# A decoder layer on one core: the state products of a chunk issued beside the output products of the chunk before it

## The chip, the cores and the metric

The kernel runs on one NeuronCore of a Trainium2 chip. The time is device microseconds of one execution; the time before is the median of three runs. A trace of one profiled execution shows every instruction of the engines: TensorE (PE, with its weight loads as PEld), VectorE (DVE), ScalarE (ACT), GpSimd (POOL), and SyncE, which starts the DMAs.

## The reference

The layer works on x of shape (4, 1024, 256): four batches, 1024 tokens, 256 channels. Its first part is a gated linear attention with 16 heads of 16 channels, whose core is a recurrence over tokens (q, k, v, beta and g come from projections of the normalised input, a rotating scan and short convolutions):

```
def step(Sst, inp):
    qt, kt, vt, bt, gt = inp
    Sd = gt[..., None, None] * Sst
    kS = jnp.einsum('bhk,bhkv->bhv', kt, Sd)
    Snew = Sd + jnp.einsum('bhk,bhv->bhkv', kt, bt[..., None] * (vt - kS))
    ot = jnp.einsum('bhk,bhkv->bhv', qt, Snew)
    return (Snew, ot)
```

The output o is normalised, gated and projected, and added to the input. The second part is a differential cross-attention over 64 context tokens. The third is a depthwise and a pointwise convolution, a mixture of 8 experts of which each token takes 2 (all 8 are computed), a normalisation and a small feed-forward layer.

## The kernel before

The 1024 tokens are worked through in 8 blocks of 128 tokens (of all four batches at once). A block passes through two halves. The first half holds projections and the recurrence; the second half holds cross-attention, experts and feed-forward. They are overlapped: the program runs through turns i from -2 to 8, and in turn i it does the recurrence of block i, the second half of block i-1 and the projections of blocks i+1 and i+2. Turns 1 to 6 are alike and are called steady here. Turn 0 has the recurrence but no second half; turn 8 has a second half alone.

The order of work on each engine is written out by hand in the table ORDERS, one list of steps for each engine and kind of turn ("head" for turns up to 0, "steady", "drain" for turn 7, "last" for turn 8). A word such as z.3 is a step with its arguments; a prefix tells the block: none is block i, - is block i-1, + is block i+1, * is block i+2. Every engine does its list strictly in order, and a step waits for semaphores of other steps: `up(name, n)` waits until event name has been counted n times, `fin` counts one. A further table, KEEP, gives how many filler products (128x128, two instructions each, into a bank that nobody reads) TensorE issues ahead of a step; they are left out while a projection is half done in the filler's bank.

The recurrence is done in 8 chunks of 16 tokens. For chunk c:
- PE z.c (L1934) forms products of the solved triangle with keys and queries in banks 2 and 3, and DVE zc.c (L1405) puts them into slot c % 4 of zc_ring.
- PE d1.c (L1951) multiplies keys with the state of the chunk before, in banks 0 and 1, and DVE m.c (L1415) makes rq, slot c % 2, from it and the values.
- PE cs.c (L1967), the state products, go to banks 0 and 1 in two halves, cs.c.0 and cs.c.1. A product takes 32 rows and 64 columns of the array. Half 0 uses the row quarters 0 and 2, half 1 the quarters 1 and 3, in both column halves: eight products or 16 instructions on four pieces of the array. Two row quarters mustn't write one bank at a time, so half 1 waits for the end of half 0. DVE s.c (L1422, four instructions) then makes the new state, for which d1.(c+1) waits.
- PE co.c (L1983), the output products, have the same shape and two halves in banks 2 and 3. They wait until zc has read z.(c+3) from these banks and until o.(c-1) is done. DVE o.c (L1433 and three at L1436) sums them up. z.(c+4) waits for o.c.

So a chunk has four halves one after another: co.(c-1).0, co.(c-1).1, cs.c.0, cs.c.1, with other work between some of them.

Other steps that the text speaks of: PE pv and DVE av (attention), PE wp and DVE wp (L1550, projection of the attention), turn4 (a turn by TensorE, copied by ScalarE), DVE dconv (L1564, L1569, depthwise convolution) for PE pw, router, PE moe.0 to moe.31 (L2132, experts, with a bias product at L1700), ScalarE moe (L1037), DVE acc (L1634, weighted sum over the experts), turn5, mi and mo (their output projection), hnorm (ScalarE L1046, L771, L772, then DVE L1644), turn6, ffd and ffu (feed-forward), turn1 (L1784, the input of block i+2 turned; copies L801 and L1229), and onorm, og, wo (output of the recurrence).

Of the kernel before, what the change touches and what calls it, by code (L numbers as in the profile page):

```python
# [105 lines left out]
def steps(words):  # L106

    out = []
    for word in words.split():
# [13 lines left out]
        -pt.12 -pt.13 -pv.6.0 -pv.6.1 -turn3.0 -pt.14 -pt.15 -wp.0.0 -wp.0.1 -pv.7.0 -pv.7.1 cs.0.0 cs.0.1 z.2
        +proj.3.0 z.3 d1.1 co.0.0 co.0.1 cs.1.0 cs.1.1 -turn4.0 z.4 d1.2 co.1.0 co.1.1 cs.2.0 cs.2.1 +proj.3.1 z.5
        d1.3 co.2.0 -turn3.1 -wp.1.0 co.2.1 cs.3.0 cs.3.1 +proj.4.0 +proj.4.1 z.6 d1.4 co.3.0 co.3.1 cs.4.0 +proj.5.0
        +proj.5.1 cs.4.1 -wp.1.1 -pw.0.0 -pw.0.1 z.7 -turn4.1 d1.5 -router.0 -moe.0 co.4.0 co.4.1 -moe.1 -pw.1.0
        cs.5.0 -pw.1.1 -moe.2 -moe.3 -router.1 -moe.4 -moe.5 -moe.6 -moe.7 -moe.8 -moe.9 -moe.10 -moe.11 -moe.12
        cs.5.1 -moe.13 -moe.14 -moe.15 -moe.16 -moe.17 -moe.18 -moe.19 -turn5.0 -moe.20 -mo.0.0 -mo.0.1 -moe.21
        -moe.22 -moe.23 -moe.24 -moe.25 -moe.26 -moe.27 -moe.28 -moe.29 co.5.0 -moe.30 -moe.31 -mi d1.6 co.5.1
        -turn5.1 cs.6.0 cs.6.1 *turn1.0 *turn1.1 co.6.0 d1.7 co.6.1 cs.7.0 cs.7.1 co.7.0 co.7.1 -turn6.0 -mo.1.0  # L130
        -mo.1.1 -ffd.0 -turn6.1 -ffu.0 -ffd.1 onorm.0 *rot.0 onorm.1 wo.0 *rot.1 wo.1 *gate.0 wo.2 -ffu.1 *unrot
        +sum.0 +sum.1'''),
        "dve": steps('''
        dsel.0 -ln2.0.0 -ln2.0.1 -ln2.1.0 -ln2.1.1 -max.0.0 -max.0.1 dsel.1 norm.0 gsub.0 gsub.1 norm.1 norm.2.0
        norm.2.1 -max.1.0 -max.1.1 norm.3.0 norm.3.1 am.0 am.1 +cond am.2 am.3 solve.0.0 -av.0.0 -av.0.1 solve.0.1
        solve.1.0 solve.1.1 solve.2.0 -av.0.2 -av.0.3 -max.2.0 -max.2.1 +db -av.1.0 -av.1.1 -av.1.2 -av.1.3 -max.3.0
        -max.3.1 -av.2.0 -av.2.1 solve.2.1 -av.2.2 -av.2.3 -max.4.0 -max.4.1 -av.3.0 -av.3.1 -av.3.2 -av.3.3 -max.5.0
        -max.5.1 solve.3.0 solve.3.1 solve.4.0 -av.4.0 -av.4.1 solve.4.1 solve.5.0 -av.4.2 -av.4.3 -anorm.0.0
        solve.5.1 solve.6.0 solve.6.1 solve.7.0 -anorm.0.1 -max.6.0 -max.6.1 -av.5.0 -av.5.1 -av.5.2 +btr -av.5.3
        solve.7.1 solve.8.0 solve.8.1 -max.7.0 -max.7.1 -av.6.0 solve.9.0 -av.6.1 -av.6.2 solve.9.1 solve.10.0  # L140
# [2125 lines left out]
```

How the kernel before makes its waits and increments, by code:

```python
    def wait(self, step=None):  # L92
        step = self.count if step is None else step
        self.eng.wait_ge(self.sem, self.i * self.per + step if self.per else step)
# [518 lines left out]
        @block.sync  # L614
# [11 lines left out]
            load_weights(["cin"], ld_cin)
            load_scratch(ramp, "ramp", ld_ramp)
            sp.dma_start(bias_row, biases[:, :]).then_inc(ld_b, 16)
            load_weights(["dw", "ctrl"], ld_proj)
            for n, name in enumerate(("wk", "wv", "ctx")):
                load_scratch(stage[:, 512 * n:512 * n + 512], name, ld_ctx)
            load_scratch(stage[:, 2048:3072], "ctxd", ld_ctx)
            load_weights(["wo", "ffu"], ld_rest)
            sp.wait_ge(su["split"], 1)
            for n in range(3):
                sp.dma_start(bias3[n:n + 1, :].rearrange("o (p n) -> o p n", p=NBR), bias_part[n]).then_inc(ld_b3, 16)
# [7 lines left out]
            def store(n):  # L647
                sp.wait_ge(ev["done"].sem, ev["done"].at(n, 2))
                sp.dma_start(rows(out, n).rearrange("b p d -> p b d"), ot[:, :, :]).then_inc(x_out.sem, 16)
# [1 line left out]
            def load_residual(i):  # L652
                sp.wait_ge(ev["tinv"].sem, ev["tinv"].at(i))
                load(xres, xres_in, i)
# [1 line left out]
            def values(i):  # L657
                sp.wait_ge(ev["vt_sb"].sem, ev["vt_sb"].at(i, 2))
                if i:
                    sp.wait_ge(v_in.sem, v_in.at(i - 1, 64))
                    sp.wait_ge(ev["r"].sem, ev["r"].at(i - 1, 8))
# [31 lines left out]
                def fin(name, ins):  # L694
                    ins.then_inc(ev[name].sem, 1)
```

## Time and profile before

| | us |
|---|---|
| median of three runs | 1506.36 (1505.03 to 1511.72) |
| the profiled execution | 1503.68, span 1501.7 |
| PE busy | 1427.1 (95%) |
| DVE busy | 1183.4 (79%) |
| ACT busy | 834.3 (56%) |
| POOL busy | 210.6 (14%) |
| chain that ended last | PE 81%, DVE 10%, ACT 6% |
| state products, L1967 | 2048 instructions, 58.9 busy |
| output products, L1983 | 2048 instructions, 58.9 busy |

Busy time is the time in which an engine had an instruction under way, so products that overlap count once. The chain follows the work back from the last instruction, at each step to what released it. The mean granted clock of TensorE is 0.992 of full speed.

### The profile page before, as it was taken

What the parts mean: (1) busy time and instruction counts of PE and PEld (TensorE: products, weight loads), DVE (VectorE), ACT (ScalarE), POOL (GpSimd) and SP (SyncE); (2) the same over time, 40 slices, a digit from 0 to 9 for tenths busy, and PEclk for the clock granted to TensorE, in tenths of its full rate; (3) what the DMA queues carried; (4) which work ended last, traced back from release to release, by engine and by line L of the source; (5) the groups of instructions that cost most, each with busy time, mean ns of one, the idle gap of its engine ahead of it and who ended that gap; (6) DMA issues with size and microseconds to landing.
All of it is one profiled execution on the core that took longest, in us unless ns stands there. A gap on an engine that the chain in (4) does not pass through costs nothing.

```text
span 1501.7 us, 38124 instructions
## 1 busy us (share of the span) xinstructions
PE 1427.1 (95%) x15778; PEld 943.8 (63%) x15778; DVE 1183.4 (79%) x3196; ACT 834.3 (56%) x1599; POOL 210.6 (14%) x221
## 2 busy tenths in 40 slices
...
DMA packets 20212, 31.27 MB, mean 21 GB/s; under 512 B 1480, under 2 KB 17864, under 8 KB 19784
## 3 DMA queue, kind: packets, MB, share of 16 engines
...
q14 instruction: 46, 0.38, 0.1%
...
## 4 chain that ended last, share of the span: by engine, by line
PE 81%; DVE 10%; ACT 6%; issue 2%; DMA 0%; POOL 0%; SPq 0%; DVEq 0%; ACTq 0%
PE bank L2132 15%; PE bank L2070 7%; PE bank L1824 7%; PE bank L1694 6%; PE four L1915 4%; PE bank L2055 4%; PE bank L2033 4%; PE bank L1719 3%; PE bank L1827 3%; PE four L1983 3%; PE bank L1744 2%; PE four L1967 2%; PE four L1719 2%; PE bank L1700 2%; PE bank L1726 2%
## 5 line engine op out<-in xcount | busy, mean ns | idle before, releaser
L2132 PE MATMUL bank<-w_sb,cs 128*128 128x512 f32 x512 | 245.2, 597 | 0.3 <-ACT cs L1037 0.3
L744 POOL TENSOR_TENSOR decayed<-state,pk 128x512 f32<-128x512 f32 x64 | 67.7, 1058 | 842.7 <-DVE state L1422 842.7
L2132 PEld LDWEIGHTS bank<-w_sb,cs 128*128 128x128 f32 x512 | 94.6, 190 | 91.2 <-issue 83.4
L1037 ACT ACTIVATE cs<-bank 128x512 f32<-128x512 f32 x112 | 66.7, 595 | 148.8 <-PE bank L1700 126.1
L2070 PEld LDWEIGHTS bank<-vx_sb,cs 128*128 128x128 f32 x896 | 108.4, 189 | 25.9 <-ACT cs L987 16.6
L2070 PE MATMUL bank<-vx_sb,cs 128*128 128x136 f32 x896 | 119.0, 284 | 3.7 <-ACT cs L987 1.5
L987 ACT COPY cs<-bank 128x512 f32<-128x512 f32 x114 | 66.5, 583 | 94.0 <-PE bank L2055 94.0
L1824 PE MATMUL bank<-hT,w_sb 128*128 128x512 f32 (+1 forms) x224 | 109.5, 611 | 2.7 <-ACT rota L840 0.8
L1634 DVE SCALAR_TENSOR_TENSOR cs<-cs,rwt 128x256 f32<-128x256 f32 x196 | 88.8, 503 | 23.4 <-ACT cs L1037 22.2
L1281 DVE SCALAR_TENSOR_TENSOR qkv<-pre,l_sb,qkv 128x512 f32<-128x512 f32 x144 | 99.5, 747 | 0.2
L1506 DVE TENSOR_REDUCE pkc<-bank 128x8 f32<-128x512 f32 x116 | 75.1, 683 | 20.3 <-PE bank L2033 20.3
L779 ACT ACT_TABLE_LOAD x66 | 84.7, 1283 | 1.1
L979 ACT ACTIVATE cs<-cs 128x1024 f32<-128x1024 f32 x60 | 63.1, 1052 | 38.6 <-DVE cs L1512 38.6
L2055 PE MATMUL bank<-c_sb,cs 128*128 128x128 f32 x456 | 72.9, 282 | 12.1 <-ACT cs L987 6.5
L1512 DVE TENSOR_TENSOR cs<-bank,pkc 128x512 f32<-128x512 f32 x116 | 74.3, 682 | 8.4 <-PE bank L2055 8.0
L2033 PE MATMUL bank<-kbx,cs 32*128 32x256 f32 x464 | 77.1, 400 | 0.7 <-ACT cs L974 0.7
L1694 PE MATMUL bank<-cs,w_sb 128*128 128x256 f32 (+1 forms) x304 | 75.4, 387 | 0.0
L2055 PEld LDWEIGHTS bank<-c_sb,cs 128*128 128x128 f32 x456 | 48.8, 140 | 39.2 <-issue 32.1
L1422 DVE SCALAR_TENSOR_TENSOR state<-four,c_sb,decayed 128x128 f32<-128x128 f32 x256 | 71.6, 343 | 1.0 <-PE four L1967 1.0
L1915 PEld LDWEIGHTS four<-kq,shared 64*64 64x64 f32 x2048 | 63.7, 135 | 13.0 <-issue 12.9
L1915 PE MATMUL four<-kq,shared 64*64 64x48 f32 x2048 | 69.2, 219 | 1.8 <-POOL shared L726 0.8
L1436 DVE SCALAR_TENSOR_TENSOR M<-four,c_sb,M 128x128 f32<-128x128 f32 x192 | 66.8, 348 | 5.1
...
## 6 DMA issues: line engine op xcount, KB each, us to landing
...
```

The costliest lines, as they stand in the source:

```text
L779: nc.scalar.preload_act_table_set(name)
L1281: ins = stt(dst, pre[:, n % 4, :, t:TB + t], L("conv", 4 * n + t, 4 * n + t + 1), dst, ALU.mult, ALU.add)
L1506: highest[a] = link(red(mx[:, a, :], sc[a], AX.X, ALU.max))
L1634: ins = stt(comb[:, b, :], src, wgt, comb[:, b, :], ALU.mult, ALU.add)
L1694: last = mm(dst, lhs(k), rhs(k), start=k == 0, stop=k == n - 1)
L1719: last = mm(dst[:, D * n:D * n + D], lhs[:, k, b * TB:b * TB + TB], rhs[:, k, :], start=False, stop=n == 1 and k == 1)
L1824: mm(dst, ctrl[:, k, at:at + n], hT[:, k, :], start=k == 0, stop=False)
L1915: last = mm(bank[RAW[c % 4]][q, 48 * n:48 * n + 48], kqb[q, c % 2, n, :], kq[q, g, b, c, :, :].rearrange("p x t -> p (x t)"), start=True, ...
L2033: last = mm(scores(j, u, a)[:, 256 * f:256 * f + 256], qx[r:r + 32, f, b * TB:b * TB + TB], kbx[r:r + 32, f, b, :], start=True, stop=True)
L2055: last = nc.tensor.transpose(turned_bank(j, u, n)[:, h * P:h * P + P], prob[:, 4 * n + h, :], ident)
L2070: last = mm(values_bank(j)[:, 34 * h:34 * h + 136], probT_of(j, u)[:, h, :], vx_sb[:, at:at + 136], start=True, stop=True)
L2132: mm(dst, x1T[:, k, b * TB:b * TB + TB], ew[:, k, ep * 512:ep * 512 + 512], start=k == 0, stop=False)
```

## The change

co.0 to co.6 are no longer steps of their own. A half of cs.c now issues each of its state products followed by an output product of chunk c-1 of the other half, so that 32 instructions use all four row quarters and write four different banks. cs.c.0 also takes over the waits: it waits for zc up to c+3 and for o.(c-2), besides r. cs_half is counted by the last output product. The old steps co.c.0 and co.c.1 remain for chunk 7 alone, as co.0 and co.1.

```
                 def cs_(c, half):

                     if half:
                         up("cs_half", c + 1)
                     else:
                         up("r", c + 1)
-                        up("zc", c + 1)
+                        up("zc", min(c + 3, 8) if c else 1)
+                        if c > 1:
+                            up("o", c - 1)
                     for g in range(G):
                         for k in range(2):
                             for a in range(2):
...
+                                last = state_product(c, g, k, a, half)
+                                if c:
+                                    last_out = out_product(c - 1, g, k, a, 1 - half)
+                    if half == 0:
+                        fin("cs_half", last_out if c else last)
+                    else:
+                        fin("cs_ps", last)
+                        if c:
+                            fin("co_ps", last_out)
+
+                def co(half):

                     if half:
-                        up("co_half", c + 1)
+                        up("co_half")
                     else:
-                        up("zc", min(c + 4, 8))
-                        if c:
-                            up("o", c)
+                        up("o", 7)
                     for g in range(G):
                         for k in range(2):
                             for a in range(2):
...
+                                last = out_product(7, g, k, a, half)
                     fin("co_ps" if half else "co_half", last)
```

state_product and out_product are the two products of before with their operands unchanged:

```
+                def state_product(c, g, k, a, half):
+
+                    q, p_ = slice(64 * a, 64 * a + 64), slice(64 * k + 32 * half, 64 * k + 32 * half + 32)
+                    dst = bank[k][q, 0:D].rearrange("p (h n v) -> p h n v", h=4, v=DH)[:, :, 2 * g + half, :]
...
+                def out_product(c, g, k, a, half):
+
+                    q, p_ = slice(64 * a, 64 * a + 64), slice(64 * k + 32 * half, 64 * k + 32 * half + 32)
+                    dst = bank[2 + k][q, 0:D].rearrange("p (h n t) -> p h n t", h=4, t=CH)[:, :, 2 * g + half, :]
```

The lists in ORDERS lose the co steps, and other steps move, in the lists of all kinds of turn; KEEP gets other entries. In the steady turn, TensorE's list from chunk 1 on:

```
-        -sc.7.1 cs.0.0 -pt.12 cs.0.1 -pt.13 z.2 -pv.6.0 -pv.6.1 -turn3.0 z.3 d1.1 -pt.14 co.0.0 co.0.1 cs.1.0 -pt.15
-        cs.1.1 -wp.0.0 -wp.0.1 z.4 d1.2 -pv.7.0 co.1.0 co.1.1 cs.2.0 -pv.7.1 cs.2.1 +proj.3.1 z.5 d1.3 -turn4.0 co.2.0
-        co.2.1 cs.3.0 +proj.4.0 cs.3.1 +proj.4.1 -turn3.1 z.6 d1.4 -wp.1.0 -wp.1.1 co.3.0 co.3.1 -pw.0.0 -pw.0.1
-        +proj.5.0 cs.4.0 -turn4.1 +proj.5.1 -router.0 -moe.0 -moe.1 -pw.1.0 -pw.1.1 -moe.2 -moe.3 -router.1 cs.4.1
...
-        -moe.24 -moe.25 -moe.26 -moe.27 -moe.28 -moe.29 -moe.30 -moe.31 co.5.0 d1.6 -mi co.5.1 cs.6.0 cs.6.1 -turn5.1
-        -turn6.0 -mo.1.0 -mo.1.1 *turn1.0 co.6.0 d1.7 co.6.1 -ffd.0 cs.7.0 cs.7.1 co.7.0 *turn1.1 co.7.1 -turn6.1
...
+        -sc.7.0 -sc.7.1 -pt.12 cs.0.1 -pt.13 z.2 -pv.6.0 -pv.6.1 z.3 d1.1 -turn3.0 -pt.14 cs.1.0 -pt.15 cs.1.1 -wp.0.0
+        -wp.0.1 z.4 d1.2 -pv.7.0 cs.2.0 -pv.7.1 cs.2.1 +proj.3.1 z.5 d1.3 -turn4.0 cs.3.0 cs.3.1 +proj.4.0 +proj.4.1
+        -turn3.1 z.6 d1.4 -wp.1.0 -wp.1.1 -pw.0.0 -pw.0.1 +proj.5.0 +proj.5.1 cs.4.0 -turn4.1 -router.0 cs.4.1 -moe.0
+        -moe.1 -pw.1.0 -pw.1.1 -moe.2 -moe.3 -router.1 -moe.4 -moe.5 -moe.6 -moe.7 z.7 d1.5 -moe.8 -moe.9 -moe.10
+        -moe.11 -moe.12 -moe.13 -moe.14 -moe.15 -moe.16 -moe.17 -moe.18 -moe.19 cs.5.0 -turn5.0 -moe.20 cs.5.1 -mo.0.0
...
+        cs.6.0 cs.6.1 -turn5.1 -turn6.0 -mo.1.0 -mo.1.1 *turn1.0 d1.7 -ffd.0 cs.7.0 cs.7.1 co.0 co.1 *turn1.1 -turn6.1
```

VectorE's list of the steady turn, two places (m to dconv, and the last expert sums):

```
-        -ln3.0.0 o.1.0 o.1.1 -ln3.0.1 o.1.2 -av.7.0 o.1.3 -av.7.1 s.2 -av.7.2 zc.5 m.3 -av.7.3 +conv.0.2
-        o.3.0 -ln3.1.1 -x1T.0 -dconv.1.0 -dconv.1.1 o.3.1 -dconv.1.2 -x1T.1 -top.0.0 o.3.2 o.3.3 -top.1.0 s.4 -top.0.1
-        -acc.11.1 -acc.12.0 -acc.13.0 -acc.12.1 -acc.13.1 s.5 -acc.14.0 -acc.15.0 -acc.14.1 -acc.15.1 m.6 o.5.0 o.5.1
-        -hnorm.0 *ln1.1 o.5.2 o.5.3 s.6 m.7 o.6.0 o.6.1 o.6.2 o.6.3 -hnorm.1 s.7 *turn1 o.7.0 o.7.1 o.7.2 o.7.3 *rot.0
...
+        -x1T.0 o.3.0 -dconv.1.0 -dconv.1.1 -dconv.1.2 -x1T.1 -top.0.0 -top.1.0 o.3.1 o.3.2 o.3.3 s.4 -top.0.1 -top.1.1
...
+        o.4.2 -acc.13.0 -acc.12.1 -acc.13.1 o.4.3 s.5 -acc.14.0 m.6 o.5.0 o.5.1 -acc.15.0 -acc.14.1 -acc.15.1 -hnorm.0
+        *ln1.1 o.5.2 o.5.3 s.6 m.7 o.6.0 o.6.1 o.6.2 o.6.3 -hnorm.1 s.7 *turn1 o.7.0 o.7.1 o.7.2 o.7.3 *rot.0 -ffu.0
```

On ScalarE the copy of turn1 now stands ahead of that of turn6.0 (before, it stood behind ffd.0). KEEP's entries for steady turns:

```
-        22): 6, (0, -1, "moe", 30): 1, (0, -1, "sc", 6, 0): 8, (0, -1, "turn5", 1): 10, (0, 0, "co", 4, 1): 2,
-        (0, 0, "vturn"): 11, (0, 1, "proj", 1, 0): 1, (0, 2, "turn1", 0): 5, (0, 2, "turn1", 1): 5, (1, 0, "co",
-        1, 1): 3, (1, 0, "z", 3): 9, (NI - 1, -1, "pt", 5): 5, (NI - 1, -1, "pt", 6): 2, (NI - 1, -1, "pt", 7):
...
+        3, (0, 0, "vturn"): 20, (0, 1, "brep", 1): 5, (1, -1, "pt", 4): 2, (1, -1, "pv", 4, 0): 2, (1, -1, "pv",
+        5, 0): 5, (1, -1, "turn6", 0): 2, (1, 1, "gate", 1): 2, (NI - 1, -1, "pt", 5): 5, (NI - 1, -1, "pt", 8):
```

## Rows read from the trace of the kernel before

**Rows 1.** Windows, a steady turn: start:end, us, busy us (instructions) of each engine.
```profile
886.30:1058.40 172.10, 168.86 (x1914) 109.98 (x1913) 144.73 (x389) 102.82 (x199) 25.72 (x26) 1.00 0.06 17
```

**Rows 2.** Windows of ten microseconds: chunk loop, expert stage.
```profile
973.00:983.00 10.00, 9.70 (x213) 6.11 (x207) 9.55 (x28) 7.29 (x14) 2.12 (x2) 1.00 0.02 4
...
1003.00:1013.00 10.00, 10.00 (x27) 4.39 (x26) 10.00 (x26) 4.23 (x7) 0.00 (x0) 1.00 0.00 0
```

**Rows 3.** Chain of waits (start us, us, what): chunk 2, and d1.
```profile
968.81 0.43 PE four L1983 x16
...
969.29 0.40 PE four L1983 x11
...
969.75 0.18 PE four L1967 x12
969.93 1.12 PE bank L2070 x8
971.05 0.39 PE four L1967 x16
...
1037.67 0.38 PE four L1951 x32
```

**Rows 4.** Timeline (start us, us, engine, line): where co and cs meet.
```profile
969.47 0.28 PE L1967 MATMUL four<-rq,shared 32*64 32x64 f32 x3
...
969.51 0.24 PE L1983 MATMUL four<-shared,rq 32*64 32x64 f32 x4
```

**Rows 5.** Timeline, TensorE: co.3, pw.0, pw.1, mi, turn6.0, turn6.1.
```profile
982.36 1.01 PE L1983 MATMUL four<-shared,rq 32*64 32x64 f32 x32
983.30 1.99 PE L1694 MATMUL bank<-cs,w_sb 128*128 128x256 f32 x8
...
991.56 1.89 PE L1694 MATMUL bank<-cs,w_sb 128*128 128x256 f32 x8
...
1031.08 1.05 PE L2147 MATMUL bank<-c_sb,cs 128*128 128x128 f32 x8
...
1034.46 0.66 PE L1726 MATMUL bank<-c_sb,cs 128*128 128x128 f32 x4 [0.33 <-DVE cs L1644]
...
1041.63 0.66 PE L1726 MATMUL bank<-c_sb,cs 128*128 128x128 f32 x4
```

**Rows 6.** Timeline, VectorE in the chunk loop: o.0.0, m.2, o.1.0, zc.6, dconv.1.0.
```profile
963.51 0.35 DVE L1433 TENSOR_SCALAR M<-four,c_sb 128x128 f32<-128x128 f32 x1 [0.74 <-PE four L1983]
...
968.20 0.48 DVE L1415 SCALAR_TENSOR_TENSOR rq<-four,c_sb,vT 128x256 f32<-128x256 f32 x1
...
969.82 0.35 DVE L1433 TENSOR_SCALAR M<-four,c_sb 128x128 f32<-128x128 f32 x1 [0.19 <-PE four L1983]
...
980.11 0.88 DVE L1405 SCALAR_TENSOR_TENSOR shared<-four,c_sb 128x256 f32<-128x256 f32 x2 [0.38 <-PE four L1934]
...
988.65 0.74 DVE L1564 TENSOR_SCALAR cs<-fT,l_sb 128x256 f32<-128x256 f32 x2 [0.25 <-ACT fT L963]
```

**Rows 7.** Timeline, VectorE: three acc, the last four acc, hnorm.0, o.6.0.
```profile
1026.95 1.28 DVE L1634 SCALAR_TENSOR_TENSOR cs<-cs,rwt 128x256 f32<-128x256 f32 x3 [0.29 <-ACT cs L1037]
...
1029.42 2.67 DVE L1634 SCALAR_TENSOR_TENSOR cs<-cs,rwt 128x256 f32<-128x256 f32 x4
...
1033.53 0.88 DVE L1644 SCALAR_TENSOR_TENSOR cs<-bank,rstd,w_sb 128x256 f32<-128x256 f32 x2 [0.20 <-ACT rstd L772]
...
1038.59 0.34 DVE L1433 TENSOR_SCALAR M<-four,c_sb 128x128 f32<-128x128 f32 x1
1038.96 1.12 DVE L1436 SCALAR_TENSOR_TENSOR M<-four,c_sb,M 128x128 f32<-128x128 f32 x3
```

**Rows 8.** Timeline, ScalarE: the copy of turn1.
```profile
1039.97 0.56 ACT L801 COPY hT<-bank 128x512 f32<-128x512 f32 x1
```

**Rows 9.** Chain of waits: fillers in the head.
```profile
59.91 7.59 PE bank L1744 x68
```

**Rows 10.** Waits of VectorE: who for whom, us in total, times, longest.
```profile
DVE M L1433 <- PE four L1983: 11.0, 17, 3.0
```

More of the change, by code:

```diff
@@ L123 @@
[L123 to L132, printed above, removed]
-        "dve": steps('''
```

331 lines of the change are left out of this document (163 added, 168 removed), and 3 rows, old and new, of the table KEEP.

## Prediction

> **What bounds the kernel now.** Read first the windows by turn [rows 1]: a steady turn takes 172.10 us, and in it TensorE is busy for 168.86 us, VectorE for 144.73 us and ScalarE for 102.82 us. So TensorE sets the pace on average. There are six such turns, and turn 7 is one more with a chunk loop beside attention; turn 0 has the chunk loop almost alone; turn 8 has none. Read next the ten-microsecond windows [rows 2]. In the chunk loop VectorE is busy 9.55 of 10.00 us and TensorE 9.70, so there both are at their limit; in the expert stage TensorE is at 10.00 throughout. Then the chain of waits and the timelines, one steady turn in detail. I write T for 1030.1 us, where that turn's last expert product gives way to the next step, and c for a chunk.
>
> **What the products cost.** In the chain, co.1.0 takes 0.43 us and 0.04 us of waiting; co.1.1 and cs.2.0, which run into each other, take together 0.64 us (969.29 to 969.93); cs.2.1 takes 0.39 us [rows 3]. The 16 instructions of a half start over some 0.25 us, 15.6 ns apart, and the rest is the array emptying. Co in front of cs thus costs 0.43 + 0.04 + 0.64 - 0.39 = 0.72 us of TensorE. The new form issues 32 instructions in one pass, on eight pieces of the array (four row quarters by two column halves) where a half used four. Does that run at twice the rate? The old and state product d1 issues 32 instructions on eight pieces (two by four) in 0.38 us [rows 3]. And where co.1.1 and cs.2.0 overlap, all four row quarters are in flight, and nine instructions start from 969.47 to 969.54, 8 ns apart [rows 4]. So I take 0.39 us for a combined pass (0.47 where the next half stands right behind it), the same as an old half. The other end is the rate of four pieces: 32 x 15.6 ns + 0.14 = 0.64 us. Seven of eight output products of a turn are then free: at 0.72 us each, 5 us of 172, and 40 us over the eight turns that have a chunk loop, if nothing else waited. That is the ceiling. The Trainium skill ("TensorE: Matmul & The Clock Gate", section "Back-to-back issue gap") gives products of 1 to 64 columns a floor of about 25 ns each. By that estimate 32 would take 0.8 us and the merge would gain nothing; the 32 instructions of d1 in 0.38 us, 64 columns each, disagree, and the sum goes by them.
>
> **What the change delays.** The price is that the output product of chunk c-1 now ends with the state product of chunk c. VectorE takes its instructions in a fixed order, and o.(c-1) still stands ahead of s.c in it. Before, o ran beside cs; now it starts behind it. Four places follow, each reckoned against the times of before in the shown turn.
>
> *Place 1, chunk 2.* m.2 ends at 968.68. The new TensorE order then has cs.2.0, pv.7.1, cs.2.1: 0.39 + 1.12 + 0.39, and 0.1 for the signal, so o.1.0 starts at 970.7 where it started at 969.82 [rows 5, 6]. Behind it in VectorE's queue are s.2, zc.5, m.3 and the depthwise convolution, and with 9.55 of 10 us busy VectorE can't make this up: d1.3 and wp.1 come 0.9 us later. One wait of 0.38 us at zc.6 [rows 6] goes, and some is lost again at wp, so that pw.0 starts at 984.1 instead of 983.30. The four output products that TensorE has been spared by then (0.72 each, and 0.94 for co.3, which stood alone, 982.36 to 983.30 [rows 5]) are spent waiting. Chunk 1 I find even: o.0 starts 0.8 us later, but behind s.1 VectorE had then waited for TensorE's wp.0, and that wait goes.
>
> *Place 2, o.3 ahead of dconv.1.* From pw.0 TensorE goes on with pw.0 1.83, proj.5.0 1.81, proj.5.1 0.86, cs.4.0 0.39, turn4.1 0.50, router.0 0.86 and cs.4.1 0.45: it reaches 990.8. o.3.0 waits for that and ends at 991.2; dconv.1 (2.3 us without the o step that lay inside it) ends at 993.5, where it ended at 991.22, and pw.1 starts at 993.6 instead of 991.56 [rows 5, 6]. From there to T all is TensorE's, and two things are missing from it: cs.4.1 (0.39, already done) and co.4 (0.72). T moves by +2.0 - 1.1 = +0.9 us.
>
> *Place 3, o.5 ahead of the last sums of the experts.* Before, VectorE did acc.15 as soon as ScalarE delivered, and hnorm.0 waited for ScalarE until T+3.4 [rows 7]. Now m.6, o.5.0 and o.5.1 stand ahead of three acc. TensorE: d1.6 0.39, mi 1.21 (its bias 0.23 and 0.98) [rows 5], cs.6.0 0.47, cs.6.1 0.45, so T+2.5. VectorE: o.5.0, o.5.1 until T+3.3, three acc at 0.43 until T+4.6, hnorm.0 0.89 until T+5.5. turn6.0 started at T+4.36 (1034.46) [rows 5], so +1.1 us, although TensorE has less to do there. Everything behind (mo.1, turn1.0) keeps that.
>
> *Place 4, co directly behind cs.7.* s.6 ends at T+8.5 (hnorm.0, 1.3 of ln1.1, 0.7 of o.5.2 and o.5.3, 1.05), d1.7 at T+9.0. ScalarE now copies turn1 before turn6, 0.56 to 0.59 us each [rows 8], so ffd.0 has its operand at T+9.6 only, and ends at T+10.6. cs.7 takes 0.92: T+11.5. co.0 needs o.6, which needs cs.7.1: four VectorE steps, 1.35 us [rows 7], in which TensorE stands still. They end at T+13.0, co.0 and co.1 at T+13.95, turn1.1 at T+14.5. There turn6.1 starts, which started at T+11.55 (1041.63) [rows 5]: +3.0 us, place 3 included. s.7, turn1 and o.7 follow the same shift, and the next turn starts that much later, for nothing between 1042 and 1058 is idle on TensorE.
>
> **Fillers.** The table KEEP gives steady turns six small matrix products (two each ahead of gate.1, pt.4 and turn6.0) where they had none; the others of the key fall into an open proj and are left out. At 0.22 us each, two instructions at 0.11 [rows 9] (place 3 in the chain of the shown turn has room for the last two; 0.34 us of waiting after gate.1 and 0.43 us after pt take most of the others) I put them at +0.2 us, bounds 0 and 0.9.
>
> **The other turns.** Turn 0: TensorE has waits there, taking co out of the front of cs gives some 0.5 us at each of two or three chunks, and the wait for o.6 at the end takes 1.0: zero, bounds -4 and +4, as its order is changed most. Turn 7: its hnorm.0 has one o step ahead, not acc as well; the wait for o.6 is there; +1, bounds -2 and +4. Turns -2, -1 and 8 and the other moved steps (ScalarE's, one of two residual sums ahead of onorm): zero, bounds -2 and +3; they stand in gaps of their engines.
>
> **Sum.** A steady turn: 0.9 + 3.0 + 0.2 = +4.1 us. Six: 24.6; turn 7: 1.0. The profiled execution took 1503.68 us (span 1501.7 and 2.0 around it): 1529.3. The median of the runs is 2.7 above it: 1532.
>
> **Rivals.**
> - *Places 1 and 2 cost nothing* and TensorE's savings before T arrive whole: 0.72 x 4 + 0.94 = 3.8 us. Then a turn changes by -3.8 + 3.0 + 0.2 = -0.6 us: 1502, no change. For it: TensorE too is at 9.70 in those windows. Against: the 0.74 us wait for co at 963.51 [rows 6] shows that VectorE stands at these signals already. Chance 0.11.
> - *The combined pass runs at the rate of four pieces*, 0.64 us. Of 14 passes ten stand on the path (chunks 2, 4, 5, 6, 7): +2.5 us a turn, +15: 1547. The rows against it are those of 8 ns. Chance 0.10.
> - *The other side:* VectorE is so far behind at T that o.5 finds its product ready and acc.15 is late anyway. Then of the tail only the 1.35 us for o.6 stands, against 1.5 us of co.5 and co.6 spared; with 3.8 before T and the fillers, -3.7 us a turn, -22: 1484. It decides at VectorE being over 2.5 us late at T; before, it waited for ScalarE inside those last four acc [rows 7]. Chance 0.08.
> - *The forecast*, 1514 to 1543: chance 0.71.
>
> Half a per cent, 7.5 us, is about what a measurement of this kernel can tell from no change. Slower by more: 0.71 + 0.10 = 0.81, less 0.01 for the edge. Same 0.12. Faster 0.08. Beside the forecast's own range, the range for 8 in 10 reaches down to the edge of the rival of no change and up to the four-piece rate: 1506 to 1547.
>
> **What would show it.** The lines of the two products busy in the same intervals, 32 instructions of a half starting within some 0.25 us; more than 0.7 us between 32 starts would mean four pieces. TensorE's busy time falls by over 3 us in a steady turn, while the turn grows to some 176 us. VectorE's waits for the product lines at L1433 (the first step of o), 11 us in all before [rows 10], grow to 40 or more; TensorE waits for VectorE's M (o.6) ahead of the last co, 1.3 us, once a turn; turn6.0 waits 1 us or more for L1644. Wrong: a steady turn under 171 us, or o.5 starting without a wait.

## The result, and the profile after

The changed kernel takes 1571.93 us (median, 1568.31 to 1572.48), the kernel before 1505.69 beside it: ratio 1.0429, 95% interval 1.0392 to 1.0466. The forecast was 1532 us, 1506 to 1547. So the sign was right and the loss, 66 us, was two and a half times the 26 forecast. The profiled execution has a span of 1569.9 us against 1501.7. In the chain that ended last, TensorE's share is now 71% and VectorE's 21%; before they were 81% and 10%. One of the twelve runs of r1_merge_1_to_5 below took 2335.2 us at a mean granted clock of 0.55, far from all others; the ratio leaves it out, and the median of the other eleven is 1505.1 us.

Windows by turn of the changed kernel, turns 1 to 6 and then turn 7 to the end (start:end, us, TensorE busy us (instructions), granted TensorE clock as a share of 2.4 GHz, DMA share, GB/s):

```profile
200.05:384.02 183.97, 171.99 (x1922) 0.96 0.06 16
384.02:564.93 180.91, 169.09 (x1923) 0.98 0.06 16
564.93:747.55 182.62, 170.92 (x1923) 0.97 0.06 16
747.55:926.82 179.27, 167.54 (x1922) 0.99 0.06 16
926.82:1107.44 180.62, 168.91 (x1922) 0.98 0.06 16
1107.44:1285.81 178.37, 164.50 (x1900) 0.97 0.05 13
1285.81:1569.10 283.29, 256.96 (x2506) 0.96 0.04 11
```

Before, turns 1 to 5 took 172.05 to 172.08 us, turn 6 168.7, and turn 7 to the last matrix product 274.2, all at a granted clock of 1.00 [rows 1]. Two things are new: turns with the same instructions differ by up to 4.7 us, and the clock is below 1. One-microsecond windows of the tail of turn 3 (the same columns) show how it is below 1:

```profile
713.00:714.00 1.00, 0.73 (x64) 1.00 0.00 0
714.00:715.00 1.00, 0.00 (x0) 1.00 0.08 16
715.00:716.00 1.00, 0.01 (x1) 1.00 0.00 0
716.00:717.00 1.00, 1.00 (x6) 0.66 0.00 0
717.00:718.00 1.00, 1.00 (x7) 0.50 0.00 0
718.00:719.00 1.00, 1.00 (x5) 0.50 0.00 0
719.00:720.00 1.00, 1.00 (x4) 0.63 0.00 0
720.00:721.00 1.00, 1.00 (x8) 1.00 0.00 0
```

TensorE stands still for 2.1 us, and then the clock is at its lower level, 1.2 GHz, for 3.4 us (0.34 + 0.50 + 0.50 + 0.37 is 1.71 us of full-speed time lost). I call this a dip. I added up (1 - granted clock) x length over windows of 5 us. The kernel before has no dip from turn 1 to the end; the changed kernel loses 6.80, 3.45, 5.15, 1.70, 3.40 and 5.14 us in turns 1 to 6 (25.6 us) and 10.25 us behind, always near a multiple of 1.7: 15 dips in six turns (two can join to 6.8 us at the lower level). Taken off the turns' lengths this leaves 177.2, 177.5, 177.5, 177.6 and 177.2 us in turns 1 to 5: the scatter between equal turns is down to 0.4 us. I call that the net length. The Trainium skill ("TensorE: Matmul & The Clock Gate", section "HAM oscillation — how this bites in real kernels") takes the penalty of a throttled stretch as its length times one minus the ratio of the clocks; by that rule a dip costs 1.7 us, and the net lengths of this kernel agree within 0.4 us. In some turns of the runs below a dip costs less, down to 1.25 us (see **The clock**), so what is put down to dips here is an upper figure and net lengths can be some tenths too short.

The whole difference between the two profiled executions (67.8 us, to the last matrix product) is then: dips 35.9; net lengths of turns 1 to 6 31.1 (5.3 in each of 1 to 5, 4.5 in 6); turn 0 1.8; net length behind turn 6 -1.2; ahead of turn 0 0.1. It is not only this execution: mean clock and length of each run give what it lost to the clock, 42 to 47 us in the four runs of the changed kernel and 7 to 23 us in the 23 runs of the kernel before beside r1 and r2 (stages ahead of turn 1 included).

The waits of the changed kernel (who for whom, us in total, times, longest); the first answers to [rows 10]:

```profile
DVE M L1428 <- PE four L1960: 67.2, 40, 2.4
...
PE bank L1721 <- DVE cs L1629: 17.7, 13, 2.1
...
PE four L1960 <- DVE M L1431: 13.7, 8, 1.7
PE four L1929 <- DVE M L1431: 11.8, 9, 1.6
```

L1960 is the output product, L1428 the first step of o, L1431 the others. VectorE's waits for output products have grown from 11.0 to 67.2 us; TensorE waits for sums of the experts (L1629, ahead of turn5.0 and, longer, ahead of turn5.1), for o.6 (ahead of co) and for o.1 (ahead of z.5).

### The profile page after: what moved, and what is told of

Its sections match the earlier page's. It is cut to its first block, busy times and chain, and to the rows that moved or that the text cites. A ratio compares the mean times of both kernels' runs of the same rounds, so it can differ in the third digit from the quotient of the medians.

```text
span 1569.9 us, 38196 instructions
## 1 busy us (share of the span) xinstructions
PE 1432.9 (91%) x15827; PEld 945.2 (60%) x15850; DVE 1176.6 (75%) x3196; ACT 836.0 (53%) x1599; POOL 209.4 (13%) x221
## 4 chain that ended last, share of the span: by engine, by line
PE 71%; DVE 21%; ACT 5%; issue 3%; DMA 0%; POOL 0%; DVEq 0%; SPq 0%; ACTq 0%
PE bank L2142 9%; PE bank L1819 7%; PE bank L1689 7%; PE bank L2080 6%; PE bank L2043 4%; PE four L1910 4%; PE bank L2065 3%; PE bank L1822 3%; PE bank L1739 3%; PE four L1954 3%; DVE shared L1400 3%; PE bank L1714 2%; PE bank L1721 2%; DVE cs L1629 2%; PE four L1714 2%
## 5 line engine op out<-in xcount | busy, mean ns | idle before, releaser
L1032 ACT ACTIVATE cs<-bank 128x512 f32<-128x512 f32 x112 | 66.8, 597 | 146.2 <-PE bank L1695 84.3
L1629 DVE SCALAR_TENSOR_TENSOR cs<-cs,rwt 128x256 f32<-128x256 f32 x196 | 84.7, 483 | 21.0 <-ACT cs L1032 20.9
L1689 PE MATMUL bank<-cs,w_sb 128*128 128x256 f32 (+1 forms) x304 | 79.7, 399 | 14.5 <-DVE cs L1564 10.7
L1501 DVE TENSOR_REDUCE pkc<-bank 128x8 f32<-128x512 f32 x116 | 75.1, 683 | 17.9 <-PE bank L2043 17.1
L2065 PE MATMUL bank<-c_sb,cs 128*128 128x128 f32 x456 | 72.4, 281 | 8.8 <-ACT cs L982 6.8
L1954 PE MATMUL four<-rq,shared 32*64 32x64 f32 x2048 | 63.5, 235 | 17.3 <-DVE rq L1410 13.0
L1960 PE MATMUL four<-shared,rq 32*64 32x64 f32 x2048 | 65.4, 240 | 14.5 <-DVE M L1431 13.7
L1954 PEld LDWEIGHTS four<-rq,shared 32*64 32x64 f32 x2048 | 45.3, 136 | 50.0 <-DVE rq L1410 20.7
L1739 PEld LDWEIGHTS bank<-c_sb 128*128 128x128 f32 x530 | 68.4, 203 | 10.9 <-issue 10.3
L1721 PE MATMUL bank<-c_sb,cs 128*128 128x128 f32 x312 | 54.4, 301 | 20.8 <-DVE cs L1629 17.7
```

The lines of the kernel that those rows point to most:

```text
L1629: ins = stt(comb[:, b, :], src, wgt, comb[:, b, :], ALU.mult, ALU.add)
L1689: last = mm(dst, lhs(k), rhs(k), start=k == 0, stop=k == n - 1)
L1721: last = nc.tensor.transpose(dst[:, D * k + TB * n:D * k + TB * n + TB], src[:, 2 * p + n, k * P:k * P + P], ident)
L1739: mm(bank[7 if i > 0 else 6][:, 0:P], ident, ident, start=True, stop=True)
L1954: return mm(dst, zc_ring[p_, c % 4, 2 * a + g, 1, :], rq[p_, c % 2, (2 * a + g) * 64:(2 * a + g) * 64 + 64].rearrange("p (h v) -> p h v", ...
L2065: last = nc.tensor.transpose(turned_bank(j, u, n)[:, h * P:h * P + P], prob[:, 4 * n + h, :], ident)
```

## The experiments

In the table, net is the mean net length of turns 1 to 5, and the dips are the us lost in turns 1 to 6 and from turn 7 on, all from the profiled execution. Time is the median of four runs (twelve for the last two), the ratio is to the kernel before on the same chip. The profiled execution can be up to 7 us from the median (f3: 1561.2 against 1554.3), so time, net and dips of a row don't add up exactly.

| kernel | us | ratio, 95% interval | net | dips |
|---|---|---|---|---|
| before | 1505.7 | 1 | 172.1 | 0 + 0 |
| changed | 1571.9 | 1.043 (1.039 to 1.047) | 177.4 | 25.6 + 10.3 |
| e1_unmerged | 1542.5 | 1.026 (1.021 to 1.031) | 175.7 | 13.6 + 6.9 |
| e2_old_steady | 1559.2 | 1.037 (1.032 to 1.041) | 176.3 | 20.5 + 8.6 |
| e3_old_steady_tail | 1548.2 | 1.029 (1.025 to 1.034) | 175.7 | 17.1 + 6.8 |
| e4_s_first | 1634.4 | 1.086 (1.081 to 1.091) | 181.3 | 61.3 + 10.2 |
| f1_refit | 1525.2 | 1.013 (1.011 to 1.015) | 172.9 | 10.3 + 6.9 |
| f2_place1 | 1557.9 | 1.036 (1.033 to 1.039) | 177.1 | 17.1 + 6.9 |
| f3_place2 | 1554.3 | 1.033 (1.031 to 1.035) | 176.4 | 22.2 + 8.5 |
| f4_fillers | 1608.7 | 1.070 (1.068 to 1.073) | 186.8 | 10.2 + 8.6 |
| h1_old_ends | 1535.6 | 1.019 (1.016 to 1.022) | 172.9 | 13.6 + 6.8 |
| h2_new_tails | 1538.4 | 1.023 (1.019 to 1.026) | 174.3 | 6.8 + 8.6 |
| k1_tail_again | 1530.0 | 1.015 (1.010 to 1.020) | 173.0 | 15.3 + 8.5 |
| k2_drain_too | 1528.2 | 1.015 (1.010 to 1.020) | 173.0 | 15.3 + 6.8 |
| p1_fill_after | 1571.6 | 1.045 (1.041 to 1.049) | 179.9 | 13.6 + 8.6 |
| p2_fill_refit | 1551.5 | 1.032 (1.027 to 1.036) | 177.7 | 3.4 + 5.1 |
| q1_tail_fill | 1524.4 | 1.013 (1.009 to 1.016) | 174.5 | 3.4 + 6.8 |
| q2_tail | 1523.2 | 1.011 (1.007 to 1.015) | 173.4 | 6.8 + 8.5 |
| r1_merge_1_to_5 | 1505.4 | 0.999 (0.996 to 1.002) | 171.8 | 8.5 + 0 |
| r2_merge_4_5 | 1498.9 | 0.997 (0.994 to 0.999) | 171.5 | 0 + 0 |

**Merge or order?**

```
e1: cs(c, 0): output product c-1, half 0, half 1; then state product, half 0
    (orders and fillers of the changed kernel; co_half back to 8 a turn)
```

> The changed kernel with its new orders and fillers, but with the products apart again: at the place of cs.c.0 the output product of chunk c-1 runs first, as two four-row-quarter passes, and then the state product, so that VectorE's o.(c-1) can start before cs.c ends. If the loss comes from the output product ending behind cs (theory), most of it goes, although TensorE does 7 x 0.72 us more in a turn: o starts beside cs again, the waits at L1433 fall below 25 us, and what is left is the tail (ScalarE's turn1 ahead of turn6, o.5 ahead of the last sums): about 1515 to 1525 us. If the loss comes from the other steps that the new orders moved (rival), it stays: 1560 us or more, since TensorE has even more to do.

29 us came back, so with the new orders the merge costs that; 37 us stay. I expected about 15 to stay. VectorE's waits for the output product are 35.3 us (expected: under 25), and each turn has a dip:

```profile
373.53:550.86 177.33, 170.45 (x1922) 0.99 0.06 16
```

The new orders are thus slower than the old ones even for the old products: 3.6 us a turn net, and 20 us of dips. The two costs don't simply add up: with the old order in steady turns the same merge costs 54 us (e2, next, against the kernel before).

```
e2, steady turns: order of the kernel before without co.0 to co.6, no fillers
    pe:  router.0 [cs.4.1] moe.0 ...    (was behind router.1)
    dve: m.4 [ln3.1.1 x1T.0] o.3.0 ...  (were behind o.3.0)
```

> The changed kernel with merged products, but steady turns in the order of the kernel before, with only the steps moved without which nothing could run (cs.4.1 ahead of the second half's experts, ln3.1.1 and x1T.0 ahead of o.3.0), and no fillers in steady turns. By my step Place 3, o.5 no longer stands ahead of the last sums: turn6.0 starts 1.1 us earlier per turn, and ScalarE's turn6 copy is ahead of turn1 again, which together give 6 x 2 us back: 1560 us. If the moved steps were all of the loss (rival): 1510 us. If the new order was a good fit for the merged products: over 1572 us.

13 us came back, the number forecast from Place 3 and ScalarE's copy, but in part by luck: net only 1.1 us a turn instead of 2, all of it behind the mi step (29.7 us against 30.8), and the rest in dips.

```
e4, all turns: dve: ... s.c  o.(c-1).0 ...  (was o.(c-1), then s.c)
```

> The changed kernel with s.c ahead of o.(c-1) on VectorE, in all turns: the state is there 1.35 us earlier, the output steps 1.05 us later. If TensorE's loss is the wait for the state (d1 and the next cs late because o stands in front of s), 1.0 us comes back at each of chunks 2, 3, 5 and 6: about 1550 us. If it is the wait for o (z.5, co.0), it grows by 1.05 us at z.5, z.6 and co.0: about 1580 us. Even, if both wait alike: 1570 us.

All three expectations missed: 62 us slower. The move took s.c past everything that stood between o.(c-1).0 and it, in the expert stage a dozen sums, and VectorE now stands at s and waits for the state product (in turn 3 at s.1, s.2, s.4, s.6 and s.7, 1.3 to 2.4 us each):

```profile
DVE state L1417 <- PE four L1954: 65.5, 40, 2.4
```

s.4 also stands ahead of the second depthwise convolution now, so that TensorE waits 2.56 us for it at pw.1 (0.87 in the changed kernel). It is no clean test of state first, but it shows what the dips can do: 61.3 us of them, turns of up to 193 us.

```profile
207.47:400.18 192.71, 176.23 (x1923) 0.94 0.06 15
```

**The places one by one.**

```
f2: pe: cs.1.0 [cs.1.1] pt.15 ...    cs.2.0 [cs.2.1] pv.7.1 ...
```

> The changed kernel, and of its steady turns only cs.1.1 directly behind cs.1.0 and cs.2.1 directly behind cs.2.0 (pt.15 and pv.7.1 behind them). By my step Place 1 o.1.0 starts 1.1 us earlier and TensorE's wait of 1.38 us ahead of z.5 goes: some 1.4 us a turn, 1563 us against 1572. If what waits there is VectorE's sum of work and not the place of the pass, under 3 us in all.

```
f3: dve: x1T.0 dconv.1.0 .1 .2 x1T.1 [o.3.0] top.0.0 ...  (was ahead of dconv.1.0)
```

> The changed kernel, and of its steady turns only o.3.0 behind the second depthwise convolution and x1T.1, not ahead of it. By my step Place 2, pw.1 no longer waits for a convolution held up by o.3.0 (0.87 us in the trace of the changed kernel): 1.0 us a turn, 1566 us. If o.3 is then late for z.7 and d1.5, the same or slower than 1572.

```
e3 = e2 and  pe:  cs.7.1 [turn1.1 turn6.1] co.0 co.1 ffu.0
             dve: m.7 [hnorm.1] o.6.0 ...
```

> As the kernel with the old steady order, and the tail changed: hnorm.1 stands ahead of o.6 on VectorE, and turn1.1 and turn6.1 stand ahead of co.0 on TensorE, so that their work fills the time in which co.0 waits for o.6. By my step Place 4 the 1.35 us wait and the shift of turn6.1 go: 2 to 2.5 us a turn, 12 to 15 us less than the kernel with the old steady order. If the tail is not what holds the turn (rival: the waits ahead of T), under 4 us less.

f2 gave 14 us back (9 expected), f3 18 us (6 expected), e3 11 us against e2 (12 to 15 expected). Net a turn, f3 gives back 1.0 us, about its wait of 0.87, as forecast. f2 gives back 0.3 us instead of 1.4: the wait ahead of z.5 fell from 1.38 to 0.45 us, but one of 0.42 came ahead of z.4. e3 gives back 0.6 us instead of 2 to 2.5. Much of the rest is dips, which none of the three forecasts had.

```
f1 = e3 and  pe:  cs.1.1, cs.2.1, cs.3.1 each directly behind cs.1.0, cs.2.0, cs.3.0
             dve: x1T.1 [o.3.0 o.3.1] top.0.0 ...
```

> The kernel with the old steady order and the changed tail, and in its steady turns the two halves of cs.1, cs.2 and cs.3 side by side (pt.15, pv.7.1 and proj.4.0 behind them), and o.3.0, o.3.1 behind the second half of the depthwise convolution. If the output steps that wait for a late cs.c.1 hold the chunk loop (1.29 us at o.1.0, 2.21 us at o.2.0 in the trace of that kernel, 1.13 us more at pw.1), some 3.5 us a turn come back: about 1527 us, against 1548. If the waits only change place, 1545 or more. If TensorE then keeps what the merge spares it, it comes near the kernel before: 1505.

1525 us, as expected. Its turns 2 and 3 have the same instructions:

```profile
372.18:547.57 175.39, 167.49 (x1913) 0.98 0.07 17
547.57:720.43 172.86, 164.79 (x1913) 1.00 0.07 17
```

Turn 3 has no dip and TensorE is busy 4.0 us less than in a turn before (168.82), of 5 spared. It is still 0.8 us longer: ahead of the mi step it is 1.2 us shorter, and the tail behind takes 29.3 us instead of 27.3. Turn 2 has two dips (3.4 us) in its tail and is 2.5 us longer than turn 3.

**The ends, and the tail again.**

```
h1 = f1 and  turns -2 to 0, 7, 8 in the order and with the fillers of before, without co.0 to co.6
h2 = h1 and  dve: s.5 acc.14.0 [m.6] acc.15.0 .. acc.15.1 [hnorm.0 s.6] o.5.0 o.5.1 [m.7] o.5.2 o.5.3 ln1.1 hnorm.1 o.6
             pe:  mo.1.1 [d1.7] turn1.0;  turn 7 likewise
```

> The refitted kernel (merged products, 1525 us), and the turns outside the steady ones (-2 to 0, 7 and 8) in the order and with the fillers of the kernel before, without co.0 to co.6. In its trace turns 7 and 8 take 8.7 us more than before and turn 0 takes 1.2 us more. If the moved steps of those orders cost this (theory: with the products apart the same orders also cost 7.1 us in turns 7 and 8), 6 to 9 us come back: 1517 us. If it is the merge itself that costs it there (rival), at most 2 us come back: 1524 us.

> As the kernel with the old ends, and in the tails of steady turns and of turn 7 the state in front: m.6 ahead of the last sums, s.6 ahead of o.5, m.7 in the middle of o.5, d1.7 ahead of turn1.0 (turn 7: s.6 ahead of o.5, m.7 in its middle, hnorm.1 ahead of o.6, turn6.1 and cs.7 earlier). TensorE waited 0.80 us for m.6, 1.14 us for hnorm.0 and 0.24 us for the state in the tail of the refitted kernel, and a tail without such waits lets the granted clock stay up (turns with and without a dip differ there by 1.5 to 2.5 us). If both go: 2 to 3 us a turn less than the kernel with the old ends, about 1502 us, as fast as before. If hnorm.0 waits for ScalarE anyway, under 1 us a turn: 1512 us or more.

Both missed. h1 is 10 us slower than f1: turn 0 takes 124.1 us instead of 118.0, what stands ahead of it 1.6 us more, and turn 7 to the end is as long as in f1 (281.8). Up to turn 1 h1 loses 8.5 us more to dips than f1 and is 7.7 us longer, so net the two head orders are even. Steady turns, whose orders are the same in both, took 4.9 us more in this execution, 3.4 of it dips. For turn 7 the order makes no difference. Against the kernel before (274.2) f1's turns 7 and 8 are 7.6 us longer, not 8.7, and 6.8 of that are dips: net there was 0.8 us to win. In h2 I had put ln1.1 behind o.5, and turn1.0 then waited 2.6 us for it.

```
k1 = f1 and  dve: acc.14.0 [m.6] acc.15.0 .. acc.15.1 [ln1.1 hnorm.0 s.6] o.5 m.7 [hnorm.1] o.6
             pe:  turn5.1 [turn1.0] turn6.0;  act: turn5.1 [turn1] turn6.0
k2 = k1 and  turn 7: pe: cs.3.0 [cs.3.1], mi [cs.6.0 cs.6.1] turn5.1, cs.7.1 [turn6.1]; dve: as k1
```

> The refitted kernel (1525 us) with another tail in its steady turns: on VectorE m.6 behind acc.14.0, then ln1.1 where it waited for ScalarE, hnorm.0, s.6, o.5, m.7, hnorm.1, o.6; on TensorE turn1.0 ahead of turn6.0; on ScalarE the copy of turn1 ahead of that of turn6. From the traces of the two kernels run last: turn6.0 can start at 147.4 of its turn instead of 148.3, and turn6.1, which stood at 154.9, at about 153: 1 to 2 us a turn and, with TensorE's waits gone, the dips of the clock (1.5 to 2.5 us in three of six turns) too. If it is so: 1510 to 1516 us. If the tail only moves the wait to co.0 (rival), 1523 us or more.

> As the kernel with the other tail, and the same in turn 7: cs.3.1 directly behind cs.3.0, cs.6 ahead of turn5.1, turn6.1 directly behind cs.7; m.6 ahead of the last sums, hnorm.0 and s.6 ahead of o.5, hnorm.1 ahead of o.6. Turns 7 and 8 took 8.7 us more than before in the refitted kernel. If waits like those in a steady turn make this, 4 to 6 us come back beside the kernel with the other tail; if it is not in these places, under 2 us.

k1 is not faster than f1 (its rival), and k2 is within 2 us of k1. k1's tail without a dip is as long as f1's (29.3 us, its turn 1): turn1.0 now waits 2.0 us for ln1.1, and with a dip behind it the tail takes 30.6 us.

**The clock.**

```
f4 = changed and KEEP: z.5: 16, pw.0: 8, turn5.0: 8, turn5.1: 20
p1 = changed and KEEP: turn5.1: 20
p2 = f1 and      KEEP: cs.6.0: 12, turn6.0: 18
```

> The changed kernel, and in its steady turns small matrix products that nobody reads ahead of the steps that wait: 16 ahead of z.5, 8 ahead of pw.0, 8 ahead of turn5.0, 20 ahead of turn5.1. If idle TensorE costs a second time, by the lower granted clock behind it (theory: turns 1 to 6 differ by 178.4 to 183.9 us with the same work and waits; the one with the fewest dips among turns 1 to 5 took 179.3), 1.7 us a turn come back: about 1562 us. If the dips only take the place of waiting (rival): 1570 to 1576 us.

> The changed kernel, with 20 small matrix products in steady turns ahead of turn5.1 only, where TensorE waits 2.12 us for the last sums; they fit into the wait. In the trace of the changed kernel the granted clock is down to 1.2 GHz in many stretches of 3.4 us behind idle stretches, each worth 1.7 us of full-speed work: 25.6 us in turns 1 to 6, 10.3 us in turn 7 and behind. Theory (the clock is the part of the loss that my sum had no term for): with half of the idle stretch gone fewer dips follow in the tail; 4 to 10 us come back, 1562 to 1568 us. Rival (the dips fall into time that TensorE would wait anyway): 1570 us or more.

> The refitted kernel (1525 us; 10.3 us of lost clock in turns 1 to 6) with 12 small products ahead of cs.6.0 and 18 ahead of turn6.0 in steady turns, where TensorE waits 0.80 and 1.14 us. Theory: the dips in the tails go, 5 to 10 us come back: 1515 to 1520 us. Rival: 1525 us or more.

No median came out by its theory (p1 and p2 by their rivals, f4 above both), and by one mistake: a filler is two instructions, so 20 of them don't fit into 2.12 us. In p2, in turn 4 (timeline: start us, us):

```profile
874.54 2.84 PE L1738 MATMUL bank<-c_sb 128*128 128x128 f32 x24
```

12 fillers take 2.84 us, 0.24 each. The views still separate the two effects in part. In p1 20 fillers (4.6 us) in a wait of 2.1 should make a turn 2.5 us longer net; it went from 177.4 to 179.9. The dips of turns 1 to 6 fell from 25.6 to 13.6 us. +15.0 - 12.0 + (dips behind) - 1.7 is +1.3, and the time is the same as without fillers (1571.6 against 1571.9). All four runs of p1 lost less to the clock (27 to 33 us) than any of the changed kernel (42 to 47). And the dips went where the fillers stand: behind turn5.1 the changed kernel has a dip in four of six turns, p1 in none. Nine microseconds from 150 us of the turn, turn 3, changed and then p1:

```profile
714.93:723.93 9.00, 7.16 (x92) 0.81 0.00 0
...
712.54:721.54 9.00, 8.22 (x92) 1.00 0.01 2
```

Two turns of p1:

```profile
379.34:562.54 183.20, 173.93 (x1965) 0.98 0.06 16
...
925.99:1106.14 180.15, 170.90 (x1965) 1.00 0.06 16
```

Equal work, two dips (3.4 us) or none, 3.05 us apart. In p2 the dips fell from 10.3 to 3.4 us, for 4.8 us a turn of overrun; but its profiled execution is the best of its four, and over all four p2 lost 15 to 28 us to the clock, f1 20 to 26, so p2's other runs don't bear the fall out. In f4 they fell to 10.2 (all four runs 24 to 32 us), at 9.4 us a turn: 52 fillers, some of which also waited for the filler's bank (1.45 and 1.15 us a turn). So by p1 and f4 an idle stretch filled takes away the dips behind it. A dip costs at most the 1.7 us that it seems to: 1.5 each in these two turns, 1.25 each in k1's tails (29.3 us without, 30.6 with), where less is waited for behind it. And fillers cost more than they bring here.

```
q2 = f1 and  dve: acc.14.0 [m.6] .. acc.15.1 [o.5.0 o.5.1 hnorm.0 s.6 ln1.1] o.5.2 o.5.3 [m.7 hnorm.1] o.6
             pe:  mo.1.1 [d1.7] turn1.0;  turn 7 as in k2
q1 = q2 and  KEEP: turn6.0: 14
```

> The refitted kernel with a third tail in steady turns (m.6 behind acc.14.0; o.5.0 and o.5.1 in the wait ahead of hnorm.0; then s.6, ln1.1, the rest of o.5, m.7, hnorm.1, o.6; d1.7 ahead of turn1.0), turn 7 as in the kernel with the other drain, and 14 small products ahead of turn6.0. By the traces turn6.0 starts at 147.3 of its turn instead of 148.3 and ffu.0 at 155.3 instead of 156.5: 1.2 us a turn, 2 us in turn 7, and with the dips 5 us more: 1510 to 1515 us. Rival: the tail is held elsewhere and nothing comes back, 1523 us or more.

> As the kernel with the third tail, without its 14 small products. Theory: 3 to 6 us above it, by dips; rival: equal to it within 1.5 us.

Both stand at their rivals: f1, q1 and q2 are within 2 us of one another. q1 has no dip in turns 1 to 5 (q2 one) and pays 1.1 us a turn of fillers for it. The four orders of the tail with cs.6 and cs.7 merged took, in turns whose tail has no dip, 29.3 us (f1, k1), 29.6 (q2) and 30.9 (h2).

**What can be kept.**

```
r1 = before and  cs(c, half) beside out(c-1, 1-half) if 1 <= i <= 6 and c in (1, 2, 3, 4, 5), else as before
     order: before, with the moves of f1 ahead of the tail (steady turns)
r2: the same with c in (4, 5), and cs.1 to cs.3 where they stood
```

> The kernel before, with products merged in steady turns only and there for chunks 1 to 5 only (cs.1 to cs.5 beside co.0 to co.4); co.5, co.6, co.7, the whole tail, and the turns -2 to 0, 7 and 8 as before. Of the steady order only what the refitted kernel had ahead of the tail is changed. In the refitted kernel the part ahead of T took 143.6 us a turn against 144.8 before, the tail 29.3 to 31.8 against 27.3, and the clock lost 1.7 us at a time behind its waits. If those parts are independent: 1.2 us a turn less than before, 1498 us. If waits in the chunk loop bring dips of the clock even so (rival): 1505 to 1512 us.

> As the kernel merged for chunks 1 to 5, but merged for chunks 4 and 5 only: co.3 and co.4 (0.94 and 0.72 us of TensorE) go into cs.4 and cs.5, in the stretch where TensorE sets the pace and VectorE has time before anybody needs o.3 and o.4. Chunks 1 to 3 keep the old form, so that no new wait stands in the chunk loop. Theory: 1.6 us a turn less than before, six turns: 1496 us. If o.3 behind the convolution delays z.7 or the sums (rival): 1503 to 1508 us.

r2 beats both kernels: 0.9965 of before, 0.9944 to 0.9985, 6.6 us by the medians. Between runs at the same mean clock (0.995) it is 3.2 us faster, 0.2%, which is what the turns give below; the rest is that its runs lost less to the clock (0.993 against 0.991 at the median), and whether the merge did that isn't shown. r1 stands at its rival, level with the kernel before. Turns 3 and 4 of r1, then turn 3 of r2:

```profile
541.24:713.90 172.66, 167.26 (x1914) 0.99 0.06 17
713.90:885.20 171.30, 165.79 (x1913) 1.00 0.07 17
```
```profile
539.44:711.20 171.76, 167.84 (x1914) 1.00 0.07 17
```

Five merged chunks make a turn without a dip up to 0.8 us shorter than before, two make it 0.6 shorter (1.6 expected). All of the 0.6 is co.4 (0.72). co.3's 0.94 us brings nothing: where TensorE spent it before, it now waits for the first half of the depthwise convolution. r2, turn 5, pw.0:

```profile
979.58 1.78 PE L1694 MATMUL bank<-cs,w_sb 128*128 128x256 f32 x7 [0.83 <-DVE cs L1569]
```

That is 96.94 us into its turn (882.64), against 96.97 before [rows 1, 5]. r1 has further waits in the chunk loop (mostly 0.3 to 0.5 us each) and a dip in five of six turns; r2 has only this one more than before, and no dip in its profiled execution. In both, the tail takes 27.3 us, as before. The other eleven runs of r1 lie between 1495.9 us at a mean clock of 0.997 and 1509.1 at 0.988.

## Why the prediction was off, by its own steps

**The products** came out as forecast. TensorE, turn 3 of the changed kernel, the first instructions of cs.6.1 beside co.5.0:

```profile
713.38 0.27 PE L1954 MATMUL four<-rq,shared 32*64 32x64 f32 x1
713.39 0.27 PE L1960 MATMUL four<-shared,rq 32*64 32x64 f32 x1
713.39 0.27 PE L1954 MATMUL four<-rq,shared 32*64 32x64 f32 x1
713.40 0.27 PE L1960 MATMUL four<-shared,rq 32*64 32x64 f32 x1
```

The 32 of the pass start from 713.38 to 713.65, 0.27 us, so the rival of four pieces (1547) is out. Net of dips TensorE is busy 165.8 us in turn 4 (167.54 - 1.70), 3.0 less than before.

**Places 1 and 2** were right in kind and came to a good third of what they cost. Turn 3, TensorE (z.5, pw.0, pw.1, turn5.0), and VectorE's o.1.0:

```profile
652.16 0.81 PE L1929 MATMUL four<-spare,M 64*32 64x128 f32 x32 [1.38 <-DVE M L1431]
...
663.25 1.99 PE L1689 MATMUL bank<-cs,w_sb 128*128 128x256 f32 x8 [0.83 <-DVE cs L1564]
...
672.87 1.99 PE L1689 MATMUL bank<-cs,w_sb 128*128 128x256 f32 x8 [0.87 <-DVE cs L1564]
...
695.61 0.66 PE L1721 MATMUL bank<-c_sb,cs 128*128 128x128 f32 x4 [0.75 <-DVE cs L1629]
```
```profile
649.88 0.35 DVE L1428 TENSOR_SCALAR M<-four,c_sb 128x128 f32<-128x128 f32 x1 [1.29 <-PE four L1960]
```

The turn starts at 564.93. o.1.0 starts 84.95 us into it; before it was 83.49 [rows 1, 6]: +1.5, forecast +0.9. z.5, which needs o.1, waits 1.38 us; I had no such wait. pw.0 is at +1.4 (forecast +0.8) and pw.1 at +2.7 (forecast +2.0) against [rows 5]. Behind it I let everything up to T be TensorE's; but o.4 holds up a sum, and turn5.0 waits 0.75 us for it. T (the end of the last expert product, 711.15) comes at 146.2 of its turn, before at 143.8: +2.5 without any dip ahead of it, forecast +0.9.

**Places 3 and 4.** TensorE (turn5.1, turn6.0, co.0), then VectorE (o.5.0, three acc, hnorm.0):

```profile
715.99 0.85 PE L1721 MATMUL bank<-c_sb,cs 128*128 128x128 f32 x4 [2.12 <-DVE cs L1629]
...
717.49 1.06 PE L1721 MATMUL bank<-c_sb,cs 128*128 128x128 f32 x4
...
726.36 1.35 PE L1960 MATMUL four<-shared,rq 32*64 32x64 f32 x32 [1.71 <-DVE M L1431]
```
```profile
714.02 0.35 DVE L1428 TENSOR_SCALAR M<-four,c_sb 128x128 f32<-128x128 f32 x1 [1.80 <-PE four L1960]
...
714.67 1.27 DVE L1629 SCALAR_TENSOR_TENSOR cs<-cs,rwt 128x256 f32<-128x256 f32 x3
715.86 0.87 DVE L1639 SCALAR_TENSOR_TENSOR cs<-bank,rstd,w_sb 128x256 f32<-128x256 f32 x2
```

The sums end at T+4.8 (forecast 4.6), hnorm.0 at T+5.6 (forecast 5.5). What waits is turn5.1, which needs the last sum, one step earlier than the turn6.0 I named. co.0 waits 1.71 us for o.6 (forecast 1.35). From the mi step to the end of the turn it is net 3.6 us longer in turn 4 (32.58 - 1.70 against 27.30); since co.5.0 no longer stands between T and mi, that is 3.2 us from T on, as forecast with the fillers. So the steps came to +4.1 us a turn and the net length grew by 5.3, and the difference is T: 31 us in six turns instead of 25. That the tail came out right is partly luck, since another step waited there, and for longer, than the one named.

**The step that failed** is the sum itself, *A steady turn: 0.9 + 3.0 + 0.2 = +4.1 us*, with *turn 7: 1.0*: each wait was priced at its own length, and the clock was put at nothing without a reason. The waits that came (1.4 to 2.1 us of idle TensorE in places where the kernel before had at most 0.4) are followed by stretches of 3.4 us at the lower clock, and turns with the same waits lose one to four such dips. That is 25.6 us in six turns and 10.3 from turn 7 on, up to 36 of the 43 us by which the profiled execution (1571.95 us) exceeds the 1529 that I worked out for it. The second step, smaller, is T: +2.5 us a turn instead of +0.9, 6 of the 43 by the net lengths. Turn 7 to the end has net 273.0 us against 274.2 before, so its own term was -1 (forecast +1). Turn 0 took 1.8 us more (forecast 0, bounds -4 and +4).

**The other side** (VectorE late at T, so that o.5 waits for nothing) didn't come: o.5.0 waited 1.80 us. **No change** assumed that places 1 and 2 are free; they cost net 2.5 us a turn. **What would show it** came for the most part (the passes, TensorE's busy time 3.0 us lower net, VectorE's waits of 67.2 us), and neither sign of being wrong did; none of these signs could tell a loss of 26 us from one of 66.

**Open.** I can't say from these runs which idle stretches bring a dip and which don't: the wait of 2.12 us ahead of turn5.1 is followed by one in turn 3 and not in turn 5, and equal turns of one kernel have different numbers. In turn 6 of the kernel before TensorE waits 2.93 us and no dip follows. And q2 has a dip in its turn 4 70.7 us into it, with no wait longer than 0.38 us in the 15 us ahead of it; the kernel before waits there just as long, without a dip. So idle time isn't the whole rule. Why four orders of the merged tail all stay 2.0 us or more above the old one isn't settled either; r1 and r2 show only that it goes when co.5 to co.7 and the old tail order are kept; which of the two does it isn't separated.
